# Second attention layer: the output bias is added to the residual by GpSimd instead of by products with a matrix of ones

## What is computed

```python
ln_out = layernorm(hidden_states, ln1_s, ln1_b)
qkv = ln_out @ w_qkv + b_qkv
q, k, v = jnp.split(qkv, 3, axis=-1)
ctx = merge_heads(attention(split_heads(q), split_heads(k), split_heads(v), ltor_mask))
attn_out = ctx @ w_ao + b_ao
x = hidden_states + attn_out
ln_out = layernorm(x, ln2_s, ln2_b)
q = ln_out @ w_q + b_q
kv = encoder_states @ w_kv + b_kv
...
cross_out = ctx @ w_co + b_co
x = x + cross_out
ln_out = layernorm(x, ln3_s, ln3_b)
mlp_out = gelu(ln_out @ w1 + b1) @ w2 + b2
return x + mlp_out
```

## Time and profile before

| what | value |
|---|---|
| median of 3 runs | 1808.37 us (1807.98 to 1810.73) |
| the profiled execution | 1809.66 us |
| its span | 1807.9 us |
| mean granted clock of TensorE | 0.963 |
| busy PE, DVE, ACT, POOL | 94%, 67%, 59%, 9% of the span |
| bias products (L1452) | 32, 468 ns each |
| adds of the third part (L2160) | 8, 2535 ns each |

### The profile page before, as it was taken

One profiled execution on the slowest core, in us unless ns is written; L12 is line 12 of the kernel. 1 busy time (PEld: TensorE's weight loads), 2 busy tenths in 40 slices (PEclk: granted clock), 3 DMA queues, 4 the chain that ended last, 5 costly groups with the idle time before them and its releaser, 6 DMA issues.

```text
span 1807.9 us, 32767 instructions
## 1 busy us (share of the span) xinstructions
PE 1695.8 (94%) x11936; PEld 1230.8 (68%) x11936; DVE 1214.2 (67%) x2795; ACT 1064.1 (59%) x2336; POOL 165.9 (9%) x221
## 2 busy tenths in 40 slices
PE   4779999999999988999999989999998799999999
PEld 2424344444434333788889879899997689999998
DVE  6666776767676562488888888988888653333332
ACT  2346766756666575587888878888888531111111
POOL 2102111010210000001000000000000100000000
PEclk8679999999999898999999999999999899999999
DMA  6322223223222222566656767676667230000000
GB/s 164 124 83 61 95 89 98 76 90 94 79 72 72 78 63 87 140 161 175 180 153 180 193 184 204 179 192 174 177 183 188 100 115 24 24 24 24 24 24 12
DMA packets 169480, 201.64 MB, mean 112 GB/s; under 512 B 25956, under 2 KB 117220, under 8 KB 169320
## 3 DMA queue, kind: packets, MB, share of 16 engines
q1 hardware_dynamic: 169032, 199.14, 39.1%
q10 hardware_dynamic: 288, 0.39, 0.1%
HBM read 131.84 MB, written 67.63 MB: 110 GB/s over the span
## 4 chain that ended last, share of the span: by engine, by line
PE 79%; DVE 11%; ACT 5%; issue 3%; DVEq 1%; DMA 1%; POOL 0%; ACTq 0%; SPq 0%
PE c_d L2188 10%; PE c_sums L2203 10%; PE b_d L1443 8%; PE b_d L1455 8%; PE a_d L526 5%; PE a_escore L499 5%; PE b_d L1522 5%; PE a_mscore L511 3%; PE a_d L611 3%; PE a_d L603 3%; DVE a_mx L854 3%; PE b_d L1539 3%; PE b_score L1510 3%; DVE b_t L1845 2%; DVE b_t L1841 2%
## 5 line engine op out<-in xcount | busy, mean ns | idle before, releaser
L854 DVE TENSOR_REDUCE a_mx<-a_mscore 128x2 f32<-128x1024 f32 x249 | 304.4, 1223 | 120.8 <-PE a_mscore L511 118.8
L678 ACT ACTIVATE a_pt<-a_escore 128x1024 f32<-128x1024 f32 x256 | 262.2, 1024 | 163.2 <-PE a_escore L499 162.3
L1669 ACT ACTIVATE b_pr<-b_t,b_nmax 128x256 f32<-128x256 f32 x512 | 254.5, 501 | 121.6 <-DVE b_nmax L1845 121.2
L2287 ACT ACTIVATE c_gT<-c_d,c_b 128x256 f32<-128x256 f32 x128 | 53.9, 473 | 267.7 <-PE c_d L2188 267.7
L1845 DVE CUSTOM_DVE_ANT_0 b_t<-b_t,b_minus 128x256 f32<-128x256 f32 x512 | 191.1, 429 | 17.3 <-issue 0.5
L1841 DVE TENSOR_TENSOR b_t<-b_score,b_mask 128x1024 f32<-128x1024 f32 x128 | 155.0, 1211 | 54.2 <-PE b_score L1510 54.1
L2332 DVE CAST c_g_high<-c_gT 128x512 fp32r<-128x512 f32 x64 | 40.3, 630 | 172.3 <-ACT c_gT L2287 172.1
L499 PEld LDWEIGHTS a_escore<-a_qst,a_kst 50*128 50x128 f32 x512 | 50.0, 192 | 153.9 <-ACT a_pt L678 99.7
L499 PE MATMUL a_escore<-a_qst,a_kst 50*128 50x512 f32 x512 | 133.6, 518 | 22.4 <-ACT a_pt L678 20.7
L2188 PE MATMUL c_d<-c_ln_high,c_w_high 128*128 128x256 f32 x512 | 145.4, 284 | 2.4 <-DVE c_ln_low L2334 2.4
L2188 PE MATMUL c_d<-c_ln_high,c_w_low 128*128 128x256 f32 x512 | 145.6, 284 | 0.0
(11 more groups left out here) (174 smaller groups left out, 3268.8 us busy)
## 6 DMA issues: line engine op xcount, KB each, us to landing
b_qst<-b_q SPq DMA_DIRECT2D x96, 256.0 KB, 4.6
b_kst<-b_k SPq DMA_DIRECT2D x96, 256.0 KB, 6.4
b_q<-b_qparts SPq DMA_DIRECT2D x64, 256.0 KB, 4.7
b_k<-b_kparts SPq DMA_DIRECT2D x64, 256.0 KB, 3.6
a_qst<-a_q_parts SPq DMA_DIRECT2D x192, 64.0 KB, 2.2
a_kst<-a_k_parts SPq DMA_DIRECT2D x186, 64.0 KB, 2.2
a_q_parts<-a_qparts SPq DMA_DIRECT2D x32, 256.0 KB, 2.3
a_k_parts<-a_kparts SPq DMA_DIRECT2D x32, 256.0 KB, 2.4
```

Source lines behind the costliest of these rows:

```text
L678: nc.scalar.activation(pt[:, at % RING, :, :], escore[:], ACT.Exp, scale=SCALE).then_inc(exp_done.sem, 1)
L854: nc.vector.tensor_reduce(mx[:, 2 * pair:2 * pair + 2, q], maxima_bank(b, n)[:], AX_X, ALU.max).then_inc(max_done.sem, 1)
L1669: last = nc.scalar.activation(pr[:, u % 2, j, :], t[:, u % 2, j, :], ACT.Exp, scale=-1.0, bias=nmax[:, u, j:j + 1], accum_out=esum[:, u, j ...
```

## The change

`bo` now holds both biases, the same in all 128 partitions, loaded by two DMAs of 256 KB with a broadcast source. `ones`, the two memsets, ACT's two copies and DVE's subtraction are gone; `gap` keeps the place of `ones` in memory. PE's output projection starts with its first real product. GpSimd adds the bias to the residual in SBUF, 128x1024 in one instruction (`add_bias`), at position 3 of its own queue and in the next round, behind a `widen`; DVE's `residual_sum` waits for that (`r_biased`) instead of for the load.

```diff
@@ attention_layer: tiles and signals
-        bo = sb("bo", [P, 2, D], F32R)
-        ones = sb("ones", [P, P], F32R)
+        bo = sb("bo", [P, 2, D])
+        sb("gap", [P, P])
...
-        bias_set = sig("bias_set", 2)
-        bias_high = sig("bias_high", 2)
-        bias_done = sig("bias_done", 1)
+        r_biased = sig("r_biased", 1)
@@ SP
                 x_out.need(sp, v - 1, 1)
-                if v == 0:
-                    sp.wait_ge(bias_done.sem, bias_done.at(0, 1))
...
             for a, n in enumerate(("b_ao", "b_co")):
-                for row in BIAS_ROWS:
-                    load(xr[row:row + 1, a, :], W[n].rearrange("(a n) -> a n", a=1), signal=outs_in)
+                load(bo[:, a, :], W[n].rearrange("(a n) -> a n", a=1).broadcast_to([P, D]), signal=outs_in)
@@ GpSimd
-            first["finished"](pool)
-            first["stored"](pool, TAIL - 1)
-            nc.gpsimd.memset(bo[:].bitcast(F32), 0.0).then_inc(bias_set.sem, 1)
-            nc.gpsimd.memset(ones[:].bitcast(F32), 1.0).then_inc(bias_set.sem, 1)
+
+            def add_bias(v):
+                if not there(v):
+                    return
+                if v == 0:
+                    pool.wait_ge(outs_in.sem, 16 * 2)
+                pool.wait_ge(r_in.sem, r_in.at(v, 1))
+                nc.gpsimd.tensor_tensor(xr[:], xr[:], bo[:, kind(v), :].unsqueeze(1).broadcast_to([P, TT, D]),
+                                        ALU.add).then_inc(r_biased.sem, 1)
...
                 widen(*unit_at(v, p + 1))
+                if p == 3:
+                    add_bias(v - 1)
@@ TensorE, by_token
-                biased = name == "o"
-                if biased:
-                    bias_done.need(pe, 0, 1)
-                    nc.tensor.matmul(at, ones[:], bo[:, kind(v), :], start=True, stop=False)
...
-                                              start=(k == 0 and c == 0 and not biased), stop=(k == KT - 1 and c == 2))
+                                              start=(k == 0 and c == 0), stop=(k == KT - 1 and c == 2))
@@ ScalarE, position
-                if (v, p) == (0, 3):
-                    act.wait_ge(outs_in.sem, 16 * 4)
-                    act.wait_ge(bias_set.sem, 2)
-                    for row in BIAS_ROWS:
-                        nc.scalar.activation(bo[row:row + 1], xr[row:row + 1], ACT.Copy).then_inc(bias_high.sem, 1)
@@ VectorE, residual_sum and position
-                    dve.wait_ge(r_in.sem, r_in.at(v, 1))
+                    dve.wait_ge(r_biased.sem, r_biased.at(v, 1))
...
-                if (v, p) == (0, 3):
-                    dve.wait_ge(bias_high.sem, bias_high.at(0, 2))
-                    row = slice(BIAS_ROWS[1], BIAS_ROWS[1] + 1)
-                    nc.vector.tensor_tensor(bo[row], xr[row], bo[row].bitcast(F32), ALU.subtract).then_inc(bias_done.sem, 1)
@@ network_layer, GpSimd
                     for p in range(5, POSITIONS):
                         ahead(END, p)
+                    second["add_bias"](END)
```

More of the change, by code:

```diff
@@ L1210, in attention_layer @@
         CONSTS = 8
-        BIAS_ROWS = (0, 32)
         WEIGHTS_AT = {(0, 2): 3, (B - 2, 1): 4, (B - 2, 4): 5, (B - 2, 7): 6, (B, 6): 7}
@@ L1422, in _ @@
                     position(v, p)
-            second["gpsimd"] = position
+            second["gpsimd"], second["add_bias"] = position, add_bias
         @block.tensor
```

## The result

The changed kernel takes 1811.07 us (median of 20 runs, 1808.12 to 1814.69) where the kernel before takes 1808.33 us (20 runs). The ratio is 1.0015, with a 95% interval of 1.0008 to 1.0022. The predicted time was 1809.4 us, with 1806.5 to 1812.5 as the forecast's own range; the measured one lies in it, and within the 0.2% that the prediction called no difference. By the interval it is a small loss (1.4 to 4.0 us), 2.7 us by the medians where the sum said 1.0.

What follows compares the result with a forecast made beforehand. Even rounds were taken as bound by TensorE. Set-up -1.2, rounds 1 to 5 -2.3, tail -0.7 and masked rounds +5.2 gave +1.0 us: 1809.4 us against the median, own range 1806.5 to 1812.5, 8 in 10 within 1800.3 to 1813.0.

Steps and rivals of the forecast that it cites:

- Products: PE's output projections: 32 bias products go, 0.23 us each, 7.4 us at most; rounds 1 to 5 gain 2.3 us together.
- A: Rounds 7 to 14: mask preparation gets past the add or the hold is absorbed; -7.7 us, 1800.7 us; chance 0.25.
- The add as a wait: GpSimd's 16 adds, 2.40 us each, behind the widen of unit 4: as a wait for DVE's residual sum they cost nothing.
- The hold: Rounds 7 to 14: the add holds DVE's mask operation L1827 for 2.2 us; together +5.2 us.
- Setting the bias up: Round 0: ACT's two copies and DVE's subtraction L1917 go; L1917 stands on the chain, gain 1.2 us.
- Round 15 and the tail: Three more products off the chain, 0.7 us less; round 15's add meets only PSUM-fed or one-input DVE work.
- B: Rounds 7 to 14: holds of 3.2 us instead of 2.2, about 1817.5 us, then clock falls; with other losses, chance 0.15.
- C: Clock's fall at 790.8 us may go with DVE 1.2 us earlier: up to 2.7 us, 1806.7 us; forecast's lower tail.

Runs made afterwards that it cites:

- the kernel with neither: Changed kernel without its 16 adds, so neither bias products nor adds and the bias of both output projections left out: 1802.81 us, ratio 0.9962.
- halves beside PSUM work: Changed kernel with the add in two halves, placed where DVE waits for scores or multiplies them out of PSUM: 1803.03 us, ratio 0.9961; repeated 1802.13 us.
- one add, later: Changed kernel with the add undivided but one position later, behind the widen of unit 5: 1803.64 us, ratio 0.9966.
- halves: Changed kernel with the add in two halves of 128x512, behind the widens of units 3 and 5: 1805.29 us, ratio 0.9983.
- three small operations: Changed kernel plus one useless 128x128 DVE operation (reciprocal, multiplication by a number or product) in each of rounds 1 to 6: 1807.41 us, once.

## Why the prediction was right

The time lies in the forecast's own range, and the mechanism was the forecast's: two products less a round are a gain only where PE sets the pace, and the hold of the mask's preparation takes it back. That the sum came within 1.7 us of the measured time is in part luck, for terms were wrong in both directions. By its steps, from the first profile of the changed kernel (and the second):

- **Products**: 0.23 us each by the chain, 0.218 by the kernel with neither. The forecast excepted round 6 (nothing) and, for A, half of round 8; in the kernel with neither the gain passed there as elsewhere (0.44 and 0.41 us in the periods that end there).
- **The add as a wait**: free, as said. It takes 2.57 us instead of 2.40 in most rounds. The Trainium skill (GPSIMD Engine Reference, Engine selection) advises against such work on GpSimd because it is slower there. Of the 38 us that the prediction estimated for that case none appeared: with the add beside PSUM work the periods are those of a kernel without it.
- **The hold**: 2.2 us by the third layer's rows, 2.19 measured (2.61 - 0.42). From round 6 to round 14 the sum said +5.2 us; measured +5.10 (+5.25). Inside it two misses cancel: round 8 was no worse than its neighbours (0.65 rather than 1.06), and round 14 was (0.94 rather than 0.5). Round 14's 0.94 also hangs on the point of reading. Only the first of the two idle times that the forecast set against the hold lies before the first residual sum; counted from round 13's to the second one of round 14 (1378.68 and 1383.13 us before), it takes 43.54 us in both kernels and 42.87 with neither. By that point the round lost nothing, and the difference stands in the tail below. Rounds 2 to 6: -1.84 forecast, -2.18 (-2.21) measured, the difference being round 6.
- **Setting the bias up: the step that failed.** It read "L1917 stands on the chain, 1.22 us" and booked all of it. No gain can be seen: 0.06 us when the work is put back, where two profiles of one kernel differ by 0.6, and PE's transposes start at the same 20.15 us. The row on the chain only bounded the gain, and the next chain, ACT's, was 0.3 us behind.
- **Round 15 and the tail**: -0.7 us forecast, for three products. From round 14's first residual sum to the end of the span the changed kernel gained 0.1 us in one profile and lost 0.6 in the other, against the first of before (from the second residual sum it lost 0.9 and 1.5). What gave the products' gain back is, as far as the profiles tell, slower matmuls at 1420 us in one profile, which is chance, and in the other the hold in round 15. The prediction had said of that add that it "meets only PSUM-fed or one-input work"; it does so only when PE is slow there, in three of the six profiles with the add in this place.

The parts explain the size: forecast +1.0, the set-up's 1.2 back, 0.6 to 1.3 for the tail, less 0.4 for round 6, is +2.4 to +3.1 us against the 2.7 of the medians (interval 1.4 to 4.0).

Of the rivals, A would have needed both of the mask's operations ahead of the add; they came 0.24 us after it. In round 13 the first one did start 0.20 us ahead (1331.51 us), and the add got in behind it and held the second: to be first with one of them is not enough. Its price of 7.7 us holds once the set-up's 1.2 are taken off: with no hold ("halves beside PSUM work") the time is 1802 to 1803 us, 5.4 to 6.7 us under the kernel before. B's longer holds did not come, and PE's stall of 0.9 us is not followed by a fall of the clock (1.00 in the window above). C's 2.7 us did not come either: behind 790 us the granted clock still stands at 0.50, from 789 to 793 us.

## What to carry to other kernels

An elementwise operation on an idle GpSimd can be free or hold DVE for its full length, and the difference is which operation of DVE starts just behind it. Put it where DVE reads PSUM, takes a reciprocal or waits, and start it by DVE's own signal; here two waits and a split turned a loss of 0.15 to 0.19% into a gain of 0.3 to 0.4% with the same arithmetic. And before a row on the chain is booked as a gain, look for the next chain behind it: what the waiting engine's other input would have cost it.

## What the runs showed that was not expected

- A reciprocal of DVE with both ends in SBUF is not held by GpSimd's add (128x4 in 0.17 us, 128x128 in 0.94 us beside 2.57 us of add); a multiplication by a number and a product of two tiles of the same 128x128 are (2.42 and 2.48 us). In "one add, later" even DVE's `tensor_scalar` of 128x2 behind an add lasts 1.17 us instead of 0.17:

```profile
1404.96 1.17 DVE L2311 TENSOR_SCALAR c_vare<-c_mv 128x2 f32<-128x2 f32 x1
```

- A hold of only 0.24 us a round, on the first reduction behind the scores, costs 0.24 us in every round, through ACT and its copy of the values ("halves"), even in self rounds where DVE idles for 2 us later in the same round. Idle time behind the place where PE waits does not help.
- The state of TensorE's clock behind a pause decides in round 15 whether GpSimd's add falls on a held operation or behind it: a slower PE costs time of its own there and saves DVE a hold of 2.2 us. After the same pause of 2.0 us the clock fell in three of the five profiles that have both the pause and the add, and stayed full in two.
- Profiles of one kernel differ by 2.4 to 3.5 us at the start of the second layer's round 0 and by 1 us in 48 products behind a pause (7.47 or 8.43 us; 6.42 in "three small operations", where the clock stayed at 1.00), while most rounds between agree to 0.05 us.
